# Moving a 64-byte tensor in SBUF ahead of the mask tiles of a relational graph layer

## The chip, the cores and the metric

The kernel runs on one core of one Trainium2 chip. The metric is the device time of one execution in microseconds (us). Matmuls run on TensorE (PE in the profile, its weight loads are PEld), elementwise work on VectorE (DVE), ScalarE (ACT) and GpSimd (POOL); DMAs are issued from the SyncE queue (SPq) and, two small ones and one store, from ACT's.

## What is computed

The reference takes `x` (128 graphs of 128 nodes with 128 features, f32) and `adj` (128 graphs, 128x128, int32, every entry 0 or 1 in the drawn inputs) and adds a relational graph convolution of the normalised rows:

```python
h = jnp.maximum(_layernorm(x, axis=-1), 0.0)
def _direction(x, W, Wg, b, bg, adj, rel_ids):
    h = x @ W.T
    g = h @ Wg.T
    vals = (h[:, :, None, :] + b) * jax.nn.sigmoid(g[:, :, None, :] + bg)
    onehot = (adj[..., None] == rel_ids).astype(h.dtype)
    return jnp.einsum('bnmr,bmrd->bnd', onehot, vals)
out = _direction(h, W_fwd, Wg_fwd, b_fwd, bg_fwd, adj, 2..40)
out = out + _direction(h, W_bwd, Wg_bwd, b_bwd, bg_bwd, adj_t, 2..40)
out = out + _direction(h, W_loop, Wg_loop, b_loop, bg_loop, adj_t, [1])
x = x + relu(out)
```

With entries of 0 and 1 alone only relation 1 has edges. The kernel computes that one and watches the entries; if it finds others, a general path (not run here) does the work again.

## The kernel before

A group is 4 graphs, so there are 32 groups; loads and stores go by chunks of 2 groups (a DMA of 512 KB). All of `x` and `adj` has room in SBUF (`x_all`, `adj_all`). Each group goes through these steps:

- row statistics on DVE (L524) into `stats`; for a batch of groups (1, 1, 2, 2 and then 4 at a time) POOL makes `var_eps` (L333), `mean_neg` (L336) and, by a power of -1/2 with the tensor `minus_half` as exponent, `rstd` (L339);
- the normalised rows `xn` (L352 on POOL, L541 on DVE). In a batch of four groups POOL does 3, 4, 3 and 3 of the four graphs of each group, DVE the rest (`BATCH_SHARES`); `xn` has room for 4 groups;
- PE turns the rows, `turn_rows`: 4 transposes (L751), `xn` stationary and the identity `ident` moving;
- ACT takes the relu of these as `hT_hi` (L414), DVE the remainder as `hT_lo` (L567);
- PE makes message and gate sums, `products`: 8 matmuls of `hT_hi` with `w_hi` and `w_lo` in turn (L764, L765) and 4 of `hT_lo` with `w_hi` (L769), 256 columns each, onto biases that ACT has put into PSUM (`seed`, L421);
- ACT takes the sigmoid as `gate` (L436), DVE multiplies to the messages `vals` (L557);
- the mask, `adj` as f32, is made by POOL (L363) or, for 10 of the 32 groups, by ACT (L405);
- PE sums over edges, `aggregate`: 4 matmuls, one for each graph, with `mask` stationary and `vals` moving, 128 columns of f32. Each of the four is two weight loads and two matmul records in the trace, so there are 8 of each for a group (L786);
- DVE adds relu of this to `x_all` (L582), and the result is stored from there. ACT also passes over every chunk of `adj` once (`watch`, L442), whose sums PE adds at the very end (L811) and DVE turns into the flag (L628, L630).

PE's order is written out: in step t the transposes of group t+2, the products of group t+1, the sums of group t. POOL's order in step t: where group t+4 begins a batch, that batch's coefficients; the mask of group t+1, unless ACT makes it; `xn` of group t+4. All waits are on semaphores that count groups.

Where tensors lie: they are placed one after another in the order in which they are allocated, at multiples of 32 bytes for each partition, `x_all` at a multiple of 128. All sizes from `x_all` (65536 bytes) to `mask` are multiples of 128, so `xn`, `hT_hi`, `hT_lo`, `gate`, `vals` and `mask` (8192 bytes) all begin at 0 modulo 128. Behind `mask` follow `stats` (768 bytes), `var_eps`, `rstd`, `mean_neg` (256 each) and `minus_half` (64). So `ident`, `w_raw`, `w_hi` and `w_lo` behind it begin at 64 modulo 128. The tiles within each of these are multiples of 512 bytes.

Of the kernel before, what the change touches and what calls it, by code (L numbers as in the profile page):

```python
# [18 lines left out]
def build(nc, x, adj, W_fwd, W_bwd, W_loop, Wg_fwd, Wg_bwd, Wg_loop,  # L19
# [15 lines left out]
    BATCH = 4 * GROUP  # L35
# [9 lines left out]
    with ctx:  # L45
        def sb(name, shape, dt=FP32):
            return ctx.enter_context(nc.sbuf_tensor(name, shape, dt))
# [10 lines left out]
        hT_lo = sb("hT_lo", [128, 2, GC], FP32R)  # L58
        gate = sb("gate", [128, 2, GC])
        vals = sb("vals", [128, 2, GC])  # L60
        mask = sb("mask", [128, MASKS, GROUP * N])
        stats = sb("stats", [128, BATCH_SLOTS, BATCH // 2, 6])
        var_eps = sb("var_eps", [128, BATCH_SLOTS, BATCH])
        rstd = sb("rstd", [128, BATCH_SLOTS, BATCH])
        mean_neg = sb("mean_neg", [128, BATCH_SLOTS, BATCH])
        minus_half = sb("minus_half", [128, BATCH])
        ident = sb("ident", [128, 128])
        ones = sb("ones", [128, 128])
        w_raw = sb("w_raw", [128, 2, 128])
# [796 lines left out]
```

How the kernel before makes its waits and increments, by code:

```python
        @block.sync  # L241
# [21 lines left out]
            load_x(1)  # L263
            load_x(2)
            load_x(3)
            load_adj(0)
            for c in range(4, LOAD_AHEAD):
                load_x(c)
                load_adj(c - 3)
            for c in range(LOAD_AHEAD, CHUNKS):
                load_x(c)
                load_adj(c - 3)
                sp.wait_ge(out_ready, (c - LOAD_AHEAD + 1) * CHUNK)
                store_tile((c - LOAD_AHEAD) * CG, (c - LOAD_AHEAD) * CC, CG)
            load_adj(CHUNKS - 3)
            load_adj(CHUNKS - 2)
            load_adj(CHUNKS - 1)
            for c in range(CHUNKS - LOAD_AHEAD, CHUNKS - 2):
                sp.wait_ge(out_ready, (c + 1) * CHUNK)
                store_tile(c * CG, c * CC, CG)
            for g in range(GROUPS - 4, GROUPS - 1):
                sp.wait_ge(out_ready, g + 1)
                store_tile(g * GROUP, g * GC, GROUP)
            sp.wait_ge(out_ready, GROUPS)
            store_tile(B - GROUP // 2, (B - GROUP // 2) * D, GROUP // 2)
            sp.wait_ge(flag_ready, 1)
            with sp.If(sp.value_load(flag[0:1, 0:1], min_val=0, max_val=1) != 0):
                sp.wait_ge(stored, 16 * STORES)
                for d, (b_, bg_) in enumerate(((b_fwd, bg_fwd), (b_bwd, bg_bwd))):
# [10 lines left out]
                with sp.Fori(0, B) as b:  # L302
                    sp.wait_ge(g_stored, b * 16 + 16)
                    sp.dma_start(g_x, x[bass.ds(b, 1), :, :].rearrange("o n d -> n (o d)")
```

## Time and profile before

| | |
|---|---|
| Median of 3 runs | 104.5 us (104.45 to 105.08) |
| Profiled execution: its time | 104.03 us |
| Profiled execution: its span | 102.2 us |
| PE busy in it | 95.4 us (93%) |
| DVE, ACT, POOL busy in it | 90.1, 88.6, 85.8 us (88, 87, 84%) |

The span reaches from the first to the last instruction that the profiler saw; the 1.8 us between it and the execution's time lie around it. Times in rows count from the span's start. A matmul's row gives its whole passage, of which the next one overlaps a good part: what a stream of n matmuls costs is the distance of their starts.

### The profile page before, as it was taken

The page shows a single profiled execution, that of the slowest core. Times are in us where ns is not written, and L with a number is a line of the kernel's source. Part 1 is how long each engine was busy: PE and PEld are TensorE (multiplying, and loading weights), DVE is VectorE, ACT ScalarE, POOL GpSimd, SP SyncE. Part 2 cuts the span into 40 slices and gives each one's busy share as a digit, 9 for nine tenths or more (in the row PEclk, how much of TensorE's full clock was granted, in tenths as well). Part 3 has the DMA queues.
Part 4 walks back from the last instruction along what each step waited for, and adds up shares of the span by engine and source line. Part 5 has one row for each costly group of instructions (what it writes and reads, how often), then busy time and mean ns, then how long its engine had stood idle before and what let it go on. Part 6 is the DMA issues. An engine that isn't in the chain of part 4 may idle for free.

```text
span 102.2 us, 2493 instructions
## 1 busy us (share of the span) xinstructions
PE 95.4 (93%) x802; PEld 91.3 (89%) x802; DVE 90.1 (88%) x196; ACT 88.6 (87%) x144; POOL 85.8 (84%) x162
## 2 busy tenths in 40 slices
PE   5986899998999999999999999999999999999960
PEld 2655789797999999999999999999999999999950
DVE  2289989999999999999999999999999788777761
ACT  5075498899799998999899989998999989898990
POOL 2188999999999999999999999999999999991000
PEclk9999999999999999999999999999999999999996
DMA  1899999999999999999999999999945150606345
GB/s 50 242 319 292 290 290 290 291 293 294 293 312 298 328 328 331 311 329 322 333 282 317 271 324 316 327 292 313 345 134 157 58 151 28 184 6 205 103 140 168
DMA packets 50288, 25.45 MB, mean 249 GB/s; under 512 B 866, under 2 KB 50276, under 8 KB 50276
## 3 DMA queue, kind: packets, MB, share of 16 engines
q1 hardware_dynamic: 50000, 25.17, 88.5%
q10 hardware_dynamic: 276, 0.13, 0.4%
q8 instruction: 6, 0.10, 0.4%
q14 instruction: 6, 0.05, 0.1%
HBM read 16.91 MB, written 8.39 MB: 247 GB/s over the span
## 4 chain that ended last, share of the span: by engine, by line
PE 71%; POOL 4%; ACT 3%; issue 1%; DVE 0%; POOLq 0%
PE psum L786 23%; PE psum L764 12%; PE psum L769 12%; PE psum L765 12%; PE psum L751 11%; POOL rstd L339 3%; ACT junk L442 2%; POOL xn L352 1%; ACT gate L436 0%; PE psum L811 0%; DVE dist_sum L628 0%; DVE flag L630 0%; POOLq L362 0%
## 5 line engine op out<-in xcount | busy, mean ns | idle before, releaser
L352 POOL TENSOR_SCALAR xn<-x_all,mean_neg,rstd 128x128 f32<-128x128 f32 x101 | 44.7, 454 | 0.7 <-POOL rstd L339 0.4
L764 PE MATMUL psum<-w_hi,hT_hi 128*128 128x256 f32 x128 | 33.8, 299 | 1.3 <-DVE w_lo L589 0.9
L786 PE MATMUL psum<-vals,mask 128*128 128x128 f32 x256 | 33.6, 275 | 0.1
L421 ACT ACTIVATE psum<-bias_all 128x1024 f32<-128x1024 f32 x32 | 33.1, 1035 | 0.3 <-DVE vals L557 0.3
L786 PEld LDWEIGHTS psum<-vals,mask 128*128 128x128 f32 x256 | 31.0, 191 | 0.2 <-issue 0.2
L765 PE MATMUL psum<-w_lo,hT_hi 128*128 128x256 f32 x128 | 31.0, 277 | 0.0
L524 DVE BATCH_NORM_STATS2 stats<-x_all 128x6 f32<-128x256 f32 x64 | 23.9, 418 | 3.2 <-DMA x_all<-in_x 3.0
L764 PEld LDWEIGHTS psum<-w_hi,hT_hi 128*128 128x128 f32 x128 | 24.1, 188 | 2.0 <-DVE w_lo L589 1.1
L557 DVE TENSOR_TENSOR vals<-psum,gate 128x512 f32<-128x512 f32 (+1 forms) x33 | 21.9, 663 | 3.9 <-ACT gate L436 3.3
L339 POOL TENSOR_TENSOR rstd<-var_eps,minus_half 128x16 f32<-128x16 f32 (+2 forms) x11 | 24.5, 2225 | 0.1
L765 PEld LDWEIGHTS psum<-w_lo,hT_hi 128*128 128x128 f32 x128 | 24.2, 189 | 0.0
L567 DVE SCALAR_TENSOR_TENSOR hT_lo<-psum,hT_hi 128x512 fp32r<-128x512 f32 x32 | 21.8, 682 | 1.2 <-ACT hT_hi L414 1.1
L414 ACT ACTIVATE hT_hi<-psum 128x512 fp32r<-128x512 f32 x32 | 19.2, 600 | 3.5 <-PE psum L751 3.5
L582 DVE SCALAR_TENSOR_TENSOR x_all<-psum,x_all 128x512 f32<-128x512 f32 (+1 forms) x33 | 21.7, 662 | 0.1
L436 ACT ACTIVATE gate<-psum 128x512 f32<-128x512 f32 (+1 forms) x33 | 19.4, 587 | 1.7 <-PE psum L769 1.7
L769 PE MATMUL psum<-w_hi,hT_lo 128*128 128x256 f32 x128 | 20.2, 278 | 0.0
L751 PE MATMUL psum<-ident,xn 128*128 128x128 f32 x128 | 19.5, 275 | 0.7 <-POOL xn L352 0.4
L442 ACT ACTIVATE junk<-adj_all,minus_half 128x1024 bf16<-128x1024 int32 x16 | 18.4, 1153 | 0.0
L769 PEld LDWEIGHTS psum<-w_hi,hT_lo 128*128 128x128 f32 x128 | 17.1, 188 | 0.1
L751 PEld LDWEIGHTS psum<-ident,xn 128*128 128x128 f32 x128 | 14.7, 142 | 1.5 <-POOL xn L352 0.8
L363 POOL CAST mask<-adj_all 128x512 f32<-128x512 int32 x22 | 13.3, 611 | 0.0
L541 DVE TENSOR_SCALAR xn<-x_all,stats,rstd 128x128 f32<-128x128 f32 x27 | 8.7, 340 | 0.0
(36 smaller groups left out, 31.3 us busy)
## 6 DMA issues: line engine op xcount, KB each, us to landing
adj_all<-in_adj SPq DMA_DIRECT2D x16, 512.0 KB, 6.8
x_all<-in_x SPq DMA_DIRECT2D x15, 512.0 KB, 6.8
out<-x_all SPq DMA_DIRECT2D x14, 512.0 KB, 6.2
out<-x_all SPq DMA_DIRECT2D x3, 256.0 KB, 2.3
x_all<-in_x SPq DMA_DIRECT2D x2, 256.0 KB, 3.0
out<-x_all ACTq DMA_DIRECT2D x1, 128.0 KB, 2.5
out<-x_all SPq DMA_DIRECT2D x1, 128.0 KB, 2.6
w_raw<-in_L_gnn_W_loop SPq DMA_DIRECT2D x1, 64.0 KB, 2.5
```

What stands on the lines that cost most here:

```text
L339: pool.tensor_tensor(rstd[:, s, 0:n], var_eps[:, s, 0:n], minus_half[:, 0:n], ALU.pow).then_inc(rstd_ready, 1)
L352: last = pool.tensor_scalar(xn[:, g % XN, j * D:j * D + D], x_all[:, g * GC + j * D:g * GC + j * D + D], mean_neg[:, b % BATCH_SLOTS, k:k ...
L421: nc.scalar.activation(prod_ps[s].rearrange("p g a d -> p g (a d)"), bias_all[:, :, :].rearrange("p a d -> p (a d)").unsqueeze(1) .to_broa ...
L524: last = nc.vector.bn_stats(stats[:, b % BATCH_SLOTS, ((g - first) * GROUP + j) // 2, :], x_all[:, g * GC + j * D:g * GC + (j + 2) * D].re ...
L557: nc.vector.tensor_tensor(per_graph(vals[:, s, :])[:, some, :], prod_ps[s][:, some, 0, :], per_graph(gate[:, s, :])[:, some, :], ALU.mult) ...
L567: nc.vector.scalar_tensor_tensor(out=hT_lo[:, s, :], in0=hT_ps[s], scalar=0.0, in1=hT_hi[:, s, :].bitcast(FP32), op0=ALU.max, op1=ALU.subt ...
L582: nc.vector.scalar_tensor_tensor(out=cols, in0=sums_ps, scalar=0.0, in1=cols, op0=ALU.max, op1=ALU.add).then_inc(half_out if more else out ...
L751: last = nc.tensor.transpose(hT_ps[s][:, j * N:j * N + N], xn[:, g % XN, j * D:j * D + D], ident[:, :])
L764: nc.tensor.matmul(to, hi, w_hi[:, :], start=False, stop=False, skip_group_check=True)
L765: nc.tensor.matmul(to, hi, w_lo[:, :], start=False, stop=False, skip_group_check=True)
L769: last = nc.tensor.matmul(to, lo, w_hi[:, :], start=False, stop=True, skip_group_check=True)
L786: last = nc.tensor.matmul(to[:, j * D:j * D + D], mask[:, g % MASKS, j * N:j * N + N], vals[:, s, j * D:j * D + D], start=True, stop=True)
```

## The change

The allocation of `minus_half` ([128, 16] f32, 64 bytes for each partition) goes from behind `mean_neg` to ahead of `mask`. No instruction is added, removed or reordered.

```diff
         gate = sb("gate", [128, 2, GC])
         vals = sb("vals", [128, 2, GC])
+
+        minus_half = sb("minus_half", [128, BATCH])
         mask = sb("mask", [128, MASKS, GROUP * N])
         stats = sb("stats", [128, BATCH_SLOTS, BATCH // 2, 6])
         var_eps = sb("var_eps", [128, BATCH_SLOTS, BATCH])
         rstd = sb("rstd", [128, BATCH_SLOTS, BATCH])
         mean_neg = sb("mean_neg", [128, BATCH_SLOTS, BATCH])
-        minus_half = sb("minus_half", [128, BATCH])
         ident = sb("ident", [128, 128])
```

By the sizes above, `mask`, `stats`, `var_eps`, `rstd` and `mean_neg` move up by 64 bytes and begin at 64 modulo 128, `minus_half` moves down by 9728 bytes and begins at 0 modulo 128 as before, and all others stay where they were. Masks and messages, until now 4096 bytes apart (0 modulo 128), are 4160 apart (64 modulo 128).

## Rows read from the trace of the kernel before

**Rows 1.** The page: busy time, and the chain that ended last, by engine and line

```profile
PE 95.4 (93%) x802; PEld 91.3 (89%) x802; DVE 90.1 (88%) x196; ACT 88.6 (87%) x144; POOL 85.8 (84%) x162
...
PE 71%; POOL 4%; ACT 3%; issue 1%; DVE 0%; POOLq 0%
```

**Rows 2.** Timeline of PE, one group: start us, us, engine, line, operation [idle before]

```profile
38.25 0.60 PE L751 MATMUL psum<-ident,xn 128*128 128x128 f32 x4
38.61 0.36 PE L764 MATMUL psum<-w_hi,hT_hi 128*128 128x256 f32 x1
...
39.60 0.62 PE L769 MATMUL psum<-w_hi,hT_lo 128*128 128x256 f32 x4
40.05 1.05 PE L786 MATMUL psum<-vals,mask 128*128 128x128 f32 x8
40.94 0.60 PE L751 MATMUL psum<-ident,xn 128*128 128x128 f32 x4
```

**Rows 3.** Instructions of L786 and L751: durations ns min/median/max, first and last start us

```profile
L786 PEld LDWEIGHTS psum<-vals,mask x256: 186/192/193, 14.2 to 98.2; 128*128 128x128 f32 x128
L786 PE MATMUL psum<-vals,mask x256: 270/275/348, 14.3 to 98.3; 128*128 128x128 f32 x128
...
L751 PE MATMUL psum<-ident,xn x128: 272/273/332, 7.2 to 92.8; 128*128 128x128 f32 x128
```

**Rows 4.** Timeline of PE: filler matmuls at the start, one slower group

```profile
11.07 0.60 PE L716 MATMUL psum<-zeros 128*128 128x256 bf16 x4
...
46.36 0.66 PE L751 MATMUL psum<-ident,xn 128*128 128x128 f32 x4
...
47.80 0.63 PE L769 MATMUL psum<-w_hi,hT_lo 128*128 128x256 f32 x4
...
49.16 0.60 PE L751 MATMUL psum<-ident,xn 128*128 128x128 f32 x4
```

**Rows 5.** Timeline of POOL, one batch of four groups

```profile
63.16 2.90 POOL L339 TENSOR_TENSOR rstd<-var_eps,minus_half 128x16 f32<-128x16 f32 x1
66.01 0.61 POOL L363 CAST mask<-adj_all 128x512 f32<-128x512 int32 x1
66.61 3.14 POOL L352 TENSOR_SCALAR xn<-x_all,mean_neg,rstd 128x128 f32<-128x128 f32 x7
...
74.03 2.90 POOL L339 TENSOR_TENSOR rstd<-var_eps,minus_half 128x16 f32<-128x16 f32 x1
```

**Rows 6.** Timeline of POOL: last share of `xn` of groups 10, 18, 22, 26

```profile
34.94 0.44 POOL L352 TENSOR_SCALAR xn<-x_all,mean_neg,rstd 128x128 f32<-128x128 f32 x1
...
56.73 0.44 POOL L352 TENSOR_SCALAR xn<-x_all,mean_neg,rstd 128x128 f32<-128x128 f32 x1
...
67.60 0.44 POOL L352 TENSOR_SCALAR xn<-x_all,mean_neg,rstd 128x128 f32<-128x128 f32 x1
...
78.47 0.44 POOL L352 TENSOR_SCALAR xn<-x_all,mean_neg,rstd 128x128 f32<-128x128 f32 x1
```

**Rows 7.** Timeline of PE: transposes of groups 6, 10, 18, 22, 26, 31

```profile
24.63 0.66 PE L751 MATMUL psum<-ident,xn 128*128 128x128 f32 x4 [0.42 <-POOL xn L352]
...
35.56 0.60 PE L751 MATMUL psum<-ident,xn 128*128 128x128 f32 x4
...
57.34 0.60 PE L751 MATMUL psum<-ident,xn 128*128 128x128 f32 x4
...
68.11 0.64 PE L751 MATMUL psum<-ident,xn 128*128 128x128 f32 x4
...
79.02 0.60 PE L751 MATMUL psum<-ident,xn 128*128 128x128 f32 x4
...
92.49 0.60 PE L751 MATMUL psum<-ident,xn 128*128 128x128 f32 x4
```

**Rows 8.** The chain that ended last, its end: start us, us, what

```profile
96.53 0.25 PE psum L769 x2
96.78 0.02 issue
96.80 0.38 ACT gate L436
97.18 1.99 ACT junk L442 x3
```

## The prediction

> **What bounds the kernel now.** I read the page first: the reader is to see that PE is busy for 93% of the span and holds 71% of the chain that ended last, with POOL second at 4%, though DVE, ACT and POOL are all busy for 84% or more [rows 1]. So PE seems to be the bound, but three engines stand close behind. Then PE's timeline, for what one group costs: four transposes from 38.25, twelve product matmuls from 38.61, eight mask matmuls from 40.05, and the next transposes at 40.94 [rows 2]. The group is 40.94 − 38.25 = 2.69 us, with no idle time in it.
>
> Then POOL's timeline, which changes the picture. POOL works without a gap in batches of four groups: from the start of one `rstd` to the next it is 74.03 − 63.16 = 10.87 us [rows 5]. Four of PE's groups are 4 x 2.69 = 10.77. PE is therefore the quicker one, and must meet POOL once for each batch. The place is the first group of a batch, whose `xn` POOL can make only after the 2.90 us of `rstd` and a mask. POOL ends its share of groups 10, 18, 22 and 26 at 35.38, 57.17, 68.04 and 78.91 (start plus 0.44) [rows 6], and PE starts their transposes at 35.56, 57.34, 68.11 and 79.02 [rows 7]. The slack is 0.18, 0.17, 0.07 and 0.11 us. Where PE is known to have waited, at group 6, the page marks 0.42 us of idle [rows 7]; 0.07 at group 22 is this same meeting, since the transposes there take 0.64 where a stream without a wait takes 0.60. So 0.06 to 0.07 us from POOL's end to PE's start is the least that a hand-over takes, and PE can come earlier by 0.11, 0.10, 0 and about 0.05 us at the four places. PE has its work done when POOL lets it: over groups 6 to 26 the two together set the pace.
>
> **The change part by part.** Nothing is added or removed. What changes is the place of six tensors modulo 128 bytes or in whole.
>
> *The mask matmuls.* In a stream PE loads the mask of one matmul while the messages of the one before still flow in. Both tiles start at 0 modulo 128 and both are read as 128 f32. The eight starts to the next transposes are 40.94 − 40.05 = 0.89 us, 0.111 each [rows 2]; within the block, (1.05 − 0.275) / 7 gives the same 0.111 [rows 2, 3]. Transposes have the same amount of f32 to move, and their two operands lie 64 bytes apart modulo 128 (`xn` at 0, `ident` at 64): (0.60 − 0.273) / 3 = 0.109 [rows 2, 3]. The fillers, bf16 with 256 columns, give 0.109 too [rows 4]. So 0.109 is what a matmul of this size costs when nothing is in its way, and the masks pay 0.002 more, to which their longest common duration, 275 against 273 ns, fits [rows 3]. If 64 bytes take that away: 0.89 − 8 x 0.109 = 0.018 us for a group, 32 x 0.018 = 0.6 us if PE alone counted. Lower bound: nothing is gained. On the other side the products, whose stationary tiles (0) and moving tiles (64) already lie 64 apart, are slower than the masks, at (0.62 − 0.28) / 3 = 0.113, or (0.63 − 0.28) / 3 = 0.117 in a slower group (0.28 is the passage of one, by the shortest blocks of the timeline; the first of a block has 0.36) [rows 2, 4]. They move their columns differently (256 for one weight load of 128), so I hold the transposes to be the nearer row: 0.109. The range of a slot is 0.109 to 0.117.
>
> The Trainium skill speaks against the change here. Its page "SBUF — State Buffer", section "Who interferes with whom", says that PE has two SBUF read ports, one for the moving operand and one for weight loads, independent of each other, and that only the port pair of VectorE and GpSimd causes contention. By that rule the place of the masks doesn't matter and the sum is 0.
>
> *What PE's gain is worth.* Groups 6 to 10: 4 x 0.018 = 0.07 us earlier at group 10, within its 0.11. At group 14 PE waits again: its transposes at 46.36 took 0.66, as after a wait [rows 4], so what was gained is gone. At group 18 0.07 is within the 0.10, and at group 22 it is given back again, since there POOL's hand-over is already at its least. At group 26 0.07 meets 0.05: PE gains 0.05 and waits for some hundredths. After 79.02 no `xn` is late. On the way to the end lie the mask blocks of groups 24 to 29 (those of 30 and 31 run beside ACT's last passes), six x 0.018 = 0.11 us. The chain then goes over the last gate to ACT's passes over `adj`, 1.99 us that the change doesn't touch [rows 8]. So 0.05 + 0.11 = 0.16 us, if nothing is lost.
>
> Something may be: behind the wait at 46.36 the products ran slower. From these transposes to the next it is 49.16 − 46.36 = 2.80 us, of which 0.06 is the wait's own and 0.05 slower products, against 2.69 [rows 2, 4]. Rows at 68.11 begin such a stretch too; each lasted some three groups. If the short wait at group 26 sets this off, 0.05 + 3 x 0.05 = 0.2 us goes the other way, and the sum is 0. I take the middle, a gain of 0.1 us.
>
> *`mask` as a target, `stats`, `var_eps`, `rstd`, `mean_neg`, `minus_half`.* POOL, DVE and ACT read and write these at another 64 bytes; all rows keep their shape. The nearest rows are POOL's own, `mask` 0.61, `xn` (3.14 − 0.44) / 6 = 0.45 and `rstd` 2.90 [rows 5], which are the same for all slots of the tensors. I take 0. Since POOL sets the pace, though, nothing covers it: 0.01 us on each of the 65 `xn` steps (13 a batch, 5 batches from 24.6 to 79.0) would be 0.65 us.
>
> Sum: the profiled execution, 104.03, less 0.1 is 103.9. The median is 0.5 above that execution, so 104.4 for the median of the changed kernel. A measurement of this kernel tells about 1%, 1.04 us, from no change.
>
> **The rivals.**
>
> *A, no effect at all.* Place doesn't matter; 0.002 us is the nature of an f32 matmul with real sums against a transpose. For it: the two differ in operation as well as in place. Against it: the bf16 fillers, no transposes, have 0.109 too, and the chosen tiles are otherwise alike. Then 104.5 us. It can't be told from the forecast by time, only by the mask slot (0.111 stays). The Trainium skill's page named above, "SBUF — State Buffer", would have it so.
>
> *B, masks become slower.* 64 bytes apart is what the products have, and these pay 0.113 to 0.117 for a slot. The place is L786, all 256 matmuls. It decides from where PE's four groups exceed POOL's 10.87: (10.87 / 4 − 2.69) / 8 = 0.0034 above 0.111, so about 0.115. At 0.113 nothing is lost; at 0.117 a group is 2.69 + 8 x 0.006 = 2.74, and from group 6 to 31, 25 groups, 68.5 us instead of 92.49 − 24.63 = 67.86 [rows 7]: 0.6 slower, 105.1 us. If products stay in their slower kind throughout as well, another 0.05 for each of 25 groups, 106.4 us. For it: the products' rows. Against it: transposes, also 64 apart, are the fastest of all.
>
> *C, POOL's pace moves.* For 0.01 us less on an `xn` step POOL would no longer hold PE back, and PE with quicker masks needs 25 x (2.69 − 0.018) = 66.8 us instead of 67.86: 103.4 us is the most that can be won by all of this together. For 0.01 more it is 105.1. For it: POOL has no cover. Against it: its operands shift by whole multiples of 64 bytes, and its durations don't differ between the slots of `rstd` or `mask`.
>
> **How the numbers follow.** The forecast (masks at 0.109 or nearly, POOL holding the gain back) has 0.5, A 0.27, B 0.15, of which half costs less than 1%, and C 0.08, half to each side. Faster by over 1% needs nearly all of C's good side: 0.04. Slower by over 1% is B's far half and a bit of C: 0.09. Within 1%: 0.87. The range: forecast and A lie between 104.2 and 104.6 by their sums; the runs shown spread from 104.45 to 105.08 and the profiled one was 104.03, so I widen to 103.9 below, and to 105.3 above to take in B at 0.117.
>
> **What would show it right or wrong.** Right: mask slots at 0.109, so that a block is 0.87 us from its start to the next transposes, with durations down to about 273 ns; POOL's batch still 10.87 us; waits of PE for `xn` at groups 10, 14, 18 and 22 that are more or longer than before; group 26's transposes at 78.97 or later. Wrong: mask slots at 0.111 (A), at 0.115 or more with POOL's `xn` ready long ahead of PE (B), or a batch of POOL that isn't 10.87 (C). A time below 103.5 would mean that POOL doesn't hold PE as I read it, or that it got quicker too.

## The result, and the profile after

The changed kernel takes 105.29 us (median of 7 runs, 105.23 to 105.85), the kernel before 104.68 (7 runs, 103.92 to 105.08): the ratio is 1.0076, interval 1.0046 to 1.0106 (ratios here are formed from all runs of both kernels, and can differ from the quotient of the two medians, here 1.0058, by up to 0.003). It is slower, by less than 1% but clear of the noise, where I had forecast a tenth of a microsecond less. On a second occasion (12 runs against 35) the ratio was 1.0028, interval 1.0005 to 1.0052. The two intervals meet at about 1.005.

The page of the changed kernel's profile, the same two parts as [rows 1]:

```profile
PE 96.6 (93%) x802; PEld 92.3 (89%) x802; DVE 90.9 (88%) x196; ACT 88.7 (86%) x144; POOL 85.6 (83%) x162
...
PE 71%; POOL 4%; ACT 2%; issue 1%; DVE 0%; POOLq 0%
```

PE has 1.2 us more of busy time with the same instructions; POOL has none. One group of PE's timeline says where, as [rows 2]:

```profile
38.82 0.60 PE L752 MATMUL psum<-ident,xn 128*128 128x128 f32 x4
39.18 0.36 PE L765 MATMUL psum<-w_hi,hT_hi 128*128 128x256 f32 x1
...
40.21 0.63 PE L770 MATMUL psum<-w_hi,hT_lo 128*128 128x256 f32 x4
40.68 1.05 PE L787 MATMUL psum<-vals,mask 128*128 128x128 f32 x8
41.57 0.60 PE L752 MATMUL psum<-ident,xn 128*128 128x128 f32 x4
```

The mask block is what it was: 41.57 − 40.68 = 0.89 us. The transposes are what they were, 39.18 − 38.82 = 0.36. The products took 40.68 − 39.18 = 1.50 us, against 40.05 − 38.61 = 1.44 in [rows 2]. So the matmuls that read no mask at all became slower, and the group is 2.75 us (2.742 over many) instead of 2.69.

That slower kind of product block was in the kernel before too, behind some waits: of the 26 product blocks that follow the transposes of groups 6 to 31, 7 ran at 0.118 us a matmul, from start to start (the 0.117 that the prediction read from [rows 4]), and 19 at 0.113. In the changed kernel all 26 are of the slow kind, though two of its blocks before these ran at 0.113. The transposes of groups 6, 10, 18, 26 and 31, which answer to [rows 7] (the first row holds only two of its four matmuls):

```profile
25.06 0.44 PE L752 MATMUL psum<-ident,xn 128*128 128x128 f32 x2 [0.46 <-POOL xn L353]
...
36.09 0.60 PE L752 MATMUL psum<-ident,xn 128*128 128x128 f32 x4
...
58.02 0.60 PE L752 MATMUL psum<-ident,xn 128*128 128x128 f32 x4
...
79.96 0.60 PE L752 MATMUL psum<-ident,xn 128*128 128x128 f32 x4
...
93.67 0.60 PE L752 MATMUL psum<-ident,xn 128*128 128x128 f32 x4
```

From group 6 to 31 it is 93.67 − 25.06 = 68.61 us, against 67.86. No block of transposes after group 6 takes more than 0.60, so PE never waits again. POOL's batch is as it was, 74.33 − 63.45 = 10.88 us as against [rows 5], and its last share of `xn` for group 26 is ready at 79.09, 0.87 us ahead of PE:

```profile
63.45 2.90 POOL L340 TENSOR_TENSOR rstd<-var_eps,minus_half 128x16 f32<-128x16 f32 x1
...
74.33 2.90 POOL L340 TENSOR_TENSOR rstd<-var_eps,minus_half 128x16 f32<-128x16 f32 x1
```

```profile
78.64 0.45 POOL L353 TENSOR_SCALAR xn<-x_all,mean_neg,rstd 128x128 f32<-128x128 f32 x1
```

Of the 1.2 us between the two profiled executions (105.23 and 104.03), 0.75 arose between groups 6 and 31. Another 0.43 was there already at group 6 (25.06 against 24.63), most of it from the first transposes on (7.52 against 7.16), which hang on the first load: that part differs from run to run and isn't the change.

### The profile page after: what moved, and what is told of

Read it like the earlier page. It is cut to its first block, busy times and chain, and to the rows that moved or that the text cites. A ratio compares the mean times of both kernels' runs of the same rounds, so it can differ in the third digit from the quotient of the medians.

```text
span 103.4 us, 2493 instructions
## 1 busy us (share of the span) xinstructions
PE 96.6 (93%) x802; PEld 92.3 (89%) x802; DVE 90.9 (88%) x196; ACT 88.7 (86%) x144; POOL 85.6 (83%) x162
## 4 chain that ended last, share of the span: by engine, by line
PE 71%; POOL 4%; ACT 2%; issue 1%; DVE 0%; POOLq 0%
PE psum L787 22%; PE psum L766 12%; PE psum L765 12%; PE psum L770 12%; PE psum L752 11%; POOL rstd L340 3%; ACT junk L443 2%; POOL xn L353 1%; ACT gate L437 0%; PE psum L812 0%; DVE dist_sum L629 0%; DVE flag L631 0%; POOLq L363 0%
## 5 line engine op out<-in xcount | busy, mean ns | idle before, releaser
L765 PE MATMUL psum<-w_hi,hT_hi 128*128 128x256 f32 x128 | 34.3, 301 | 1.3 <-DVE w_lo L590 0.9
L766 PE MATMUL psum<-w_lo,hT_hi 128*128 128x256 f32 x128 | 31.5, 280 | 0.0
L542 DVE TENSOR_SCALAR xn<-x_all,stats,rstd 128x128 f32<-128x128 f32 x27 | 9.5, 370 | 0.0
```

The costliest lines, as they stand in the source:

```text
L765: nc.tensor.matmul(to, hi, w_hi[:, :], start=False, stop=False, skip_group_check=True)
L766: nc.tensor.matmul(to, hi, w_lo[:, :], start=False, stop=False, skip_group_check=True)
```

## The experiments

In each, pads are unused tensors; none changes what is computed. "Distance" below is the place of `w_hi` less that of `hT_hi`, modulo 256: it is 64 in both kernels. Everything is read from two numbers of each trace, how many of those 26 product blocks are slow (0.115 us a matmul or more), and the usual length of a group; the time is beside. There is one trace of each run.

### First: is it the masks' place, the small tensors', or chance?

`minus_half` stands ahead of `mask` as in the changed kernel, but padded, so that the masks and all behind them go up by 128 bytes and all places modulo 128 stay:

```diff
+        minus_half = sb("minus_half", [128, BATCH])
+        sb("pad0", [128, 16])
         mask = sb("mask", [128, MASKS, GROUP * N])
...
-        minus_half = sb("minus_half", [128, BATCH])
+        sb("pad1", [128, 16])
         ident = sb("ident", [128, 128])
```

> Masks, statistics and everything behind them moved up by 128 bytes, so that all places modulo 128 are those of the kernel before. Theory P (places modulo 128 decide): as the kernel before, ratio within 0.997 to 1.003, part of the product blocks at 0.113 us a matmul and part at 0.118. Theory C (the slow stretch of the changed kernel is chance, or comes with any move): anything up to 1.008. Theory N (what counts is the distance of masks and messages in whole, not modulo 128): as the changed kernel, 1.007.

1.0014 (0.9993 to 1.0034), no slow block of 26. That is neither kernel: fewer slow blocks than before the change.

The masks alone at 64 modulo 128:

```diff
+        sb("pad0", [128, 16])
         mask = sb("mask", [128, MASKS, GROUP * N])
+        sb("pad1", [128, 16])
         stats = sb("stats", [128, BATCH_SLOTS, BATCH // 2, 6])
```

> The masks alone stand at 64 modulo 128, the statistics, minus_half and all else as in the kernel before modulo 128. Theory P with the masks as the cause: 1.006 to 1.009 over before, all product blocks after group 6 at 0.118. If the small tensors are the cause: 1.000, product blocks partly at 0.113. In all theories mask matmuls stay at 0.111.

1.0007 (0.9988 to 1.0026), 5 slow blocks.

The small tensors alone (`minus_half` between `mask` and `stats`):

```diff
         mask = sb("mask", [128, MASKS, GROUP * N])
+        minus_half = sb("minus_half", [128, BATCH])
         stats = sb("stats", [128, BATCH_SLOTS, BATCH // 2, 6])
...
-        minus_half = sb("minus_half", [128, BATCH])
```

> Only stats, var_eps, rstd and mean_neg stand at 64 modulo 128; masks at 0 as before. If the masks are the cause: 1.000. If the small tensors are (over POOL's or VectorE's hand-over of the rows): 1.006 to 1.009.

1.0012 (0.9990 to 1.0033), 7 slow blocks, a group 2.694: the kernel before again.

Messages and masks both at 64 (a pad of 64 bytes ahead of `vals`, one ahead of `stats`):

> Messages and masks both at 64 modulo 128, so 0 apart between them, all else as before modulo 128. If the distance of masks and messages counts: 1.000. If the masks' own place against the products' tiles counts (the weight load of the first mask runs beside the last product, whose moving tile w_hi is at 64): 1.006 to 1.009. If it is chance: no telling.

1.0016 (0.9986 to 1.0046), 3 slow blocks.

No piece of the change was slower. Either it took all of them, or the first result was of the occasion, or something hidden differed: three of the four had pushed `ident` and `w_hi` up by 128 bytes to keep them at 64 modulo 128, and the changed kernel had not.

### Second: the changed kernel again, and its neighbours

The changed kernel as it is:

> The changed kernel as it is, timed beside the kernel before and the others of this job. If its loss belongs to its layout: 1.005 to 1.009, and product blocks at 0.118 us a matmul from group 6 to the end. If the loss was of the occasion (the chip, or how the runs fell): 1.000 to 1.003 with blocks of both kinds, as in the layouts with only the masks or only the small tensors moved.

1.0028 (1.0005 to 1.0052), all 26 blocks slow, 68.61 us from group 6 to 31, as in its first trace to the hundredth. The slow pattern belongs to the layout; how much time it costs is less sure, 0.3% here against 0.8% before.

The changed kernel, with 128 bytes of pad ahead of `ident`:

```diff
         mean_neg = sb("mean_neg", [128, BATCH_SLOTS, BATCH])
+        sb("pad0", [128, 32])
         ident = sb("ident", [128, 128])
```

> The changed layout with 128 bytes more ahead of ident, w_hi and w_lo, so that modulo 128 nothing differs from the changed kernel. Theory P2 (masks and small tensors together at 64 modulo 128 are what it takes): 1.006 to 1.009. Theory W (places in whole matter, which none of the padded layouts shared with the changed kernel): 1.000 to 1.002.

0.9999 (0.9978 to 1.0021), no slow block. Modulo 128 nothing had changed, so 128 is too small a period.

Masks and small tensors at 64 by a pad ahead of `mask` and one ahead of `minus_half`:

> Masks and small tensors at 64 modulo 128 by a pad, minus_half behind them at 0. P2: 1.006 to 1.009. If only minus_half in front of the masks matters: 1.000 to 1.002. Chance: between.

0.9986 (0.9960 to 1.0012), no slow block; here too `ident` and `w_hi` stood 128 bytes on.

The kernel before with a pad of 64 bytes ahead of `ident`, so that transposes and products have both tiles at 0 modulo 128:

> The kernel before with ident, ones, w_raw, w_hi, w_lo and all behind at 0 modulo 128, so that transposes and products read stationary and moving tile at the same place modulo 128. If the phase of the two reads decides between 0.113 and 0.118: product matmuls of one kind alone and transposes at 0.111 like the masks. If not: transposes 0.109, products of both kinds, ratio 1.000.

1.0077 (1.0045 to 1.0110), all 26 slow (0.119 us a matmul), a group 2.755. Only the products changed. The transposes, with both tiles now at the same place modulo 128, kept their pace: four of them again reach from 53.68 to the next block at 54.04, as 38.25 to 38.61 in [rows 2].

```profile
53.68 0.60 PE L752 MATMUL psum<-ident,xn 128*128 128x128 f32 x4
54.04 0.37 PE L765 MATMUL psum<-w_hi,hT_hi 128*128 128x256 f32 x1
```

### Third: the distance between w and hT

`w_hi`, `w_lo` and what lies behind them 128 bytes on; `ident`, masks and small tensors stay:

```diff
         w_gT = sb("w_gT", [128, 128])
+        sb("pad0", [128, 32])
         w_hi = sb("w_hi", [128, 2 * D], FP32R)
```

> The kernel before with w_hi, w_lo and what lies behind them 128 bytes further; masks, small tensors, ident and w_raw stay. Theory D (product matmuls go at 0.113 or 0.118 us by the distance of their stationary tile hT and their moving tile w modulo 256: 64 in the kernel before and the changed one, 192 in the four padded layouts that ran at 0.113): every product block between the first waits and the end at 0.113; time 0.998 to 1.001, since POOL holds the rest. Theory I (it was ident that mattered): blocks of both kinds as before.

0.9999 (0.9975 to 1.0023), 1 slow block of 26, so it is `w`, not `ident`. The trace shows both halves of the story, the pace without a wait (2.71 us a group) and the wait that takes it back once in each batch:

```profile
47.02 0.66 PE L752 MATMUL psum<-ident,xn 128*128 128x128 f32 x4
49.80 0.60 PE L752 MATMUL psum<-ident,xn 128*128 128x128 f32 x4
52.51 0.60 PE L752 MATMUL psum<-ident,xn 128*128 128x128 f32 x4
55.22 0.60 PE L752 MATMUL psum<-ident,xn 128*128 128x128 f32 x4
57.94 0.66 PE L752 MATMUL psum<-ident,xn 128*128 128x128 f32 x4
```

52.51 to 55.22 is 2.71; 47.02 to 57.94, one batch, is 10.92, and POOL's batches there take as long (10.91 and 10.92, against 10.87 in [rows 5]):

```profile
42.08 2.90 POOL L340 TENSOR_TENSOR rstd<-var_eps,minus_half 128x16 f32<-128x16 f32 x1
52.99 2.90 POOL L340 TENSOR_TENSOR rstd<-var_eps,minus_half 128x16 f32<-128x16 f32 x1
63.91 2.90 POOL L340 TENSOR_TENSOR rstd<-var_eps,minus_half 128x16 f32<-128x16 f32 x1
```

A product block at this distance takes 1.46 us, between the 1.45 and 1.50 of the two kinds at distance 64; its matmuls go at 0.114:

```profile
52.87 0.37 PE L765 MATMUL psum<-w_hi,hT_hi 128*128 128x256 f32 x1
...
54.33 1.05 PE L787 MATMUL psum<-vals,mask 128*128 128x128 f32 x8
```

The same distance made from the other side (a pad of 128 bytes ahead of `hT_hi`, one ahead of `gate`; `w_hi` is 256 on):

> hT_hi and hT_lo 128 bytes further, all behind them 256, so the distance of w and hT is 192 modulo 256 while w keeps its place modulo 256. Theory D: all product blocks after the first waits at 0.113. If the place of w alone matters: blocks of both kinds as before.

0.9999 (0.9971 to 1.0027), 5 slow blocks, each within three of a wait, a group 2.707. It didn't reach the expected "all at 0.113", but it has the steady group of the other layouts at distance 192 and of no other distance: the distance counts, not the place of `w` alone.

Distance 0 (a pad of 192 bytes ahead of `w_hi`):

> w_hi and w_lo 192 bytes further, so at distance 0 modulo 256 from hT (0 modulo 128, as in the run with ident and w at 0, which had distance 128 and up to 0.120 us). Theory D asks for its own figure at each distance: another than 0.118 to 0.120 here speaks for a period of 256, the same as there for one of 128.

1.0167 (1.0134 to 1.0200, from four runs), all 26 slow (0.120 us a matmul), a group 2.767; the slowest of all the layouts. Of its 69.50 us from group 6 to 31, 0.26 is a single wait, at group 30, behind an `xn` tile that took VectorE 1.50 us. So the distances modulo 256 give, by the usual group: 192, 2.707 us; 64, 2.694 or 2.742; 128, 2.755; 0, 2.767. Distances 0 and 128 differ by 0.012 us, 64 and 192 by 0.013 or more, so the period isn't 128.

```profile
50.12 0.60 PE L752 MATMUL psum<-ident,xn 128*128 128x128 f32 x4
50.48 0.36 PE L765 MATMUL psum<-w_hi,hT_hi 128*128 128x256 f32 x1
...
51.52 0.64 PE L770 MATMUL psum<-w_hi,hT_lo 128*128 128x256 f32 x4
52.00 1.06 PE L787 MATMUL psum<-vals,mask 128*128 128x128 f32 x8
```

Here, at distance 0, the products take 52.00 − 50.48 = 1.52 us, against 1.44 in [rows 2].

### Fourth: which of the change's moves matters at distance 64

The masks as in the changed kernel, `stats`, `var_eps`, `rstd` at 0 modulo 128, `mean_neg` at the end; `ident` and `w_hi` exactly where both kernels have them:

```diff
+        minus_half = sb("minus_half", [128, BATCH])
         mask = sb("mask", [128, MASKS, GROUP * N])
+        sb("pad0", [128, 16])
         stats = sb("stats", [128, BATCH_SLOTS, BATCH // 2, 6])
...
-        mean_neg = sb("mean_neg", [128, BATCH_SLOTS, BATCH])
-        minus_half = sb("minus_half", [128, BATCH])
+        sb("pad1", [128, 48])
```

> Masks as in the changed kernel, stats, var_eps and rstd at 0 modulo 128, mean_neg at the end; ident, w_hi and w_lo exactly where both kernels have them. If the masks are what keeps the products at 0.118 once w stands 64 from hT: all blocks from group 6 on at 0.118, ratio 1.003 to 1.008. If it takes the small tensors too: blocks of both kinds, 1.000.

1.0060 (1.0024 to 1.0095), all 26 slow, 68.61 us from group 6 to 31. One group of it, with a product block of 43.21 − 41.71 = 1.50 us and a mask block of 0.89:

```profile
41.71 0.36 PE L767 MATMUL psum<-w_hi,hT_hi 128*128 128x256 f32 x1
...
42.74 0.64 PE L772 MATMUL psum<-w_hi,hT_lo 128*128 128x256 f32 x4
43.21 1.05 PE L789 MATMUL psum<-vals,mask 128*128 128x128 f32 x8
44.10 0.60 PE L754 MATMUL psum<-ident,xn 128*128 128x128 f32 x4
```

With the small tensors moved alone, above, nothing had changed. So at distance 64 the masks' move is the cause, and the place of `stats`, `var_eps` and `rstd` modulo 128 has no part in it.

Masks by 128 and by 192 bytes, all behind them by 256:

> Masks 128 bytes on, all behind them 256, so that only the masks' place modulo 256 differs from the kernel before; w stays 64 from hT. If what keeps the products at 0.118 is that masks and w_hi fall on the same place modulo 256 (they do in the changed kernel), or that masks lie at 64 modulo 128: blocks of both kinds, 0.998 to 1.003. If any move of the masks does it: all blocks slow, 1.005.

> Masks at 64 modulo 128 as in the changed kernel, but 128 away from w_hi modulo 256 where the changed kernel has 0. If 64 modulo 128 is enough: all blocks slow, 1.005. If it takes the same place as w_hi modulo 256: blocks of both kinds, 1.000.

By 128: 0.9991 (0.9958 to 1.0024), 11 slow blocks, in four stretches of two or three, each behind a wait. By 192: 1.0053 (1.0023 to 1.0083), all 26 slow. So at distance 64 it is enough that the masks lie at 64 modulo 128; that they fell on the place of `w_hi` modulo 256 doesn't matter, nor does `minus_half`, which stands behind the masks here as in the kernel before. And `w_hi` lies 256 bytes farther from `hT_hi` in these two, without another pace of the products: 256 is enough as the period.

### Fifth: was POOL's pace what hid the faster products?

One of a batch's tiles from POOL to VectorE, in both kernels:

```diff
-    BATCH_SHARES = (3, 4, 3, 3)
+    BATCH_SHARES = (3, 3, 3, 3)
```

> The kernel before with one row tile in four groups moved from POOL to VectorE (shares 3, 3, 3, 3). POOL's batch falls from 10.87 to 10.44 us, below PE's 10.77, so PE no longer waits for xn after group 6 or so, and with no wait the slow stretches don't come back. If POOL held PE in the kernel before: 25 groups at 2.693 instead of 67.9 us, 0.993 to 0.997. If POOL never held it: 1.000 or, by VectorE's 0.34 us more a batch, above.

> The same in the changed kernel. If PE itself is its bound, at 2.741 us a group and with POOL ahead: 1.005 to 1.008 over before, nothing gained by the relief, and 1.008 to 1.012 between this and the relieved kernel before. If POOL had been the cause of its loss: below 1.002.

The kernel before so altered: 1.0055 (1.0024 to 1.0086), not the gain I expected. The changed kernel: 1.0148 (1.0117 to 1.0180). Between the two it is 106.33 / 105.35 = 1.0093, within what I had put down. The middle of their traces is as expected, the kernel before so altered first, the changed one second:

```profile
41.20 0.60 PE L751 MATMUL psum<-ident,xn 128*128 128x128 f32 x4
...
57.36 0.60 PE L751 MATMUL psum<-ident,xn 128*128 128x128 f32 x4
```

```profile
41.84 0.60 PE L752 MATMUL psum<-ident,xn 128*128 128x128 f32 x4
...
55.55 0.60 PE L752 MATMUL psum<-ident,xn 128*128 128x128 f32 x4
```

With no wait for POOL, six groups of the one take 16.16 us (2.693 each) and five of the other 13.71 (2.742): the two paces bare. But VectorE had no room for the tile. It was busy without a gap, fell behind, and PE waited for it: at 60.13 for an `xn` tile that took 0.88 us, where 0.34 is usual, and again at 68.72 and 80.04. What hid the gain had only changed its name. With the waits the slow blocks came back, 9 of the next 10; they make 11 of 26 in all.

```profile
59.15 0.88 DVE L541 TENSOR_SCALAR xn<-x_all,stats,rstd 128x128 f32<-128x128 f32 x1
```

```profile
60.13 0.63 PE L751 MATMUL psum<-ident,xn 128*128 128x128 f32 x4
```

So I took work from POOL that no other engine has to do: the mean straight out of `stats`, with a subtraction, instead of `mean_neg` and an addition (the instruction that makes `mean_neg` and the waits for it go too).

```diff
-                        mean_neg[:, b % BATCH_SLOTS, k:k + 1], rstd[:, b % BATCH_SLOTS, k:k + 1],
-                        ALU.add, ALU.mult)
+                        stats[:, b % BATCH_SLOTS, k // 2, 1 + k % 2 * 3:2 + k % 2 * 3],
+                        rstd[:, b % BATCH_SLOTS, k:k + 1], ALU.subtract, ALU.mult)
```

> The kernel before without mean_neg: POOL subtracts the mean out of stats, as VectorE does already. That takes 0.29 us from each of POOL's batches, 10.87 to 10.58, and gives no other engine more work. PE at 2.69 us a group (10.77 for four) is then the slowest; no waits for xn after group 6, so product blocks fall to 0.113 within a few groups and stay. If POOL held the kernel before: transposes of group 31 come 0.3 to 0.5 us earlier after those of group 6 than 67.9 us, ratio 0.995 to 0.998. If POOL didn't: 1.000.

> The same in the changed kernel. Product blocks stay at 0.118 and PE was its bound already: no gain, 1.004 to 1.007 over before, from group 6 to group 31 68.5 us as in the changed kernel. A gain like that of the kernel before would mean that POOL held the changed kernel too.

Both expectations were missed, and neither run tells what it was made for; they are at 1.291 and 1.290 (135.14 and 134.91 us). A tile of `xn` took POOL 792 ns instead of 446:

```profile
L348 POOL TENSOR_SCALAR xn<-x_all,stats,rstd x101: 785/792/951, 8.1 to 122.3; 128x128 f32<-128x128 f32 x101
```

They give one thing: where POOL is far behind everybody, the two layouts take the same time. A version that beats both kernels was not found. The layout with `w_hi` 128 bytes on has no lasting slow stretch and, as POOL holds it, the time of the kernel before.

## Why the prediction was wrong

**The step that failed** was in "The mask matmuls": the change was taken to act on the matmuls that read a mask, and the slow kind of product block was taken for something that waits start and that ends by itself. So the products stood in the sum with at most 3 x 0.05 us, behind one wait; they cost 0.05 us in every group from 6 to 31. I had both kinds of block before me and tied the slow one to waits alone. Rival B ends with "if products stay in their slower kind throughout as well": they did, and the masks' own part of B, 0.117 a slot, did not happen. B's add-on of 0.05 on 2.69 makes 2.74 us a group and 68.5 us from group 6 to 31; measured 68.61.

**The mask slot** was to go from 0.111 to 0.109. It stayed at 0.111 in both kernels and was, by the median, between 0.111 and 0.112 in all 18 further runs, with masks 0, 64, 128 or 192 from the messages modulo 256. My evidence was that transposes, 64 apart, cost 0.109; with both tiles at 0 they still cost 0.109. The comparison was of two operations, as rival A said, not of two places. Rival A was right on the slot and wrong on the sum.

**The Trainium skill's rule** ("SBUF — State Buffer", "Who interferes with whom": TensorE's two read ports are independent, and only VectorE's and GpSimd's shared pair contends) agrees with the mask slots. What the prediction drew from it, that place doesn't matter, fails at the products. Moving nothing but tensors changed a group from 2.707 to 2.767 us by the distance of stationary and moving tile. The measurement decides: here the place of TensorE's own two operands matters, by up to 0.06 us in 2.7. Whether the two reads meet at a port or elsewhere no run shows.

**POOL as the second bound** was right. Its batch stayed at 10.88, so rival C fell. The layouts with no slow block (1.0014, 0.9999, 0.9986) are no faster than the kernel before, and their PE waits once in each batch. This is why the loss isn't larger: PE's own pace fell by 2.742 − 2.693 = 0.049 us a group, 1.2 us over 25, but the kernel before couldn't use the faster pace beyond 10.87 a batch. Against 67.86, 68.61 is 0.75 us; the ratios of the two occasions make 0.3 and 0.8. With POOL relieved the two layouts lay 0.93% apart.

**The waits** were to become longer; behind group 6 they vanished, as the bound passed from POOL to PE. **The small tensors** at nothing: right, shown by the run with them alone and the one with the masks alone. **The range** held the median, 105.29 us, by luck: its upper end of 105.3 was there for masks at 0.117 a slot, and the masks didn't slow down.

What stays open: why masks at 64 modulo 128 keep the products, which don't read them, in the slow kind. The start of a product block seems to inherit something from the blocks ahead of it: after a wait the kernel before has two or three slow blocks and then falls back without any wait, the changed one, from group 6 on, never does. What this something is, no run here shows.

## What to carry to other kernels

When the address of a tile moves, look at every matmul of the stream, not only at those that read it. Where a stream of the same instructions goes at two paces in the trace before, a change can pin it to one of them, and both ends belong in the sum. Price a gain on one engine against the slack of the next: here one tile of 0.34 us moved to VectorE, or 0.05 us a group off the products, met another engine at once.

## What the runs showed that I had not expected

- The distance modulo 256 between the stationary and the moving tile of the 256-column matmuls sets their pace: the usual group was 2.707 us at 192, 2.694 or 2.742 at 64, 2.755 at 128 and 2.767 at 0. The worst layout, at distance 0, is at 1.0167 in time, one wait of 0.26 us included.
- At distance 64 there are two paces for the same instructions, 0.113 and 0.118 us a matmul. Which holds was reproducible: 26 of 26 slow in both traces of the changed kernel, 68.61 us in each.
- On GpSimd, a 128x128 f32 `tensor_scalar` with a subtraction and its operand out of `stats` took 792 ns, with an addition out of `mean_neg` 446. The runs don't separate the operation from the operand's place; VectorE has the same form at 340.
- VectorE's `xn` tile, 0.34 us as a rule, took 0.88 in a stretch where it ran beside POOL's mask and `xn` instructions; with one more such tile in four groups, 5 of 34 took 0.75 to 0.88.
